# Two score groups ahead of a tile's value chunks, another place for the modulation lines, and another order of VectorE's statistics, in an attention and FP4 feed-forward block

## What is computed

```python
mod = (silu(c) @ wmod).reshape(B, 6, 1, D)
sa, ca, ga, sb, cb, gb = (mod[:, i] for i in range(6))
ga, gb = (gates pushed away from zero, to at least 0.25 in size)
h = layernorm(x) * (1 + ca) + sa
q, k, v = h @ query_proj, h @ key_proj, h @ value_proj
sim = einsum('bnkh,bmhk->bnhm', q, k) / 4
attn = softmax(sim, axis=1)                 # over n, the queries
x = x + ga * (attn @ v) @ output_proj
h = layernorm(x) * (1 + cb) + sb
x = x + gb * ffn(h)                         # silu(gate) * up, FP4-rounded operands
```

## Time and profile before

| | us |
|---|---|
| median of 3 runs | 1777.58 (1774.27 to 1778.04) |
| the profiled execution | 1776.08 |
| its span in the profile | 1774.8 |
| TensorE busy | 1687.0 (95%) |
| VectorE busy | 1663.4 (94%) |
| ScalarE busy | 1368.5 (77%) |
| GpSimd busy | 500.3 (28%) |

### The profile page before, as it was taken

How to read it: one execution, slowest core, us unless ns; L and a number is a source line. 1 busy time by engine, 2 the same in 40 slices (tenths; PEclk the granted TensorE clock), 3 DMA queues, 4 the chain that set the end, 5 groups by cost and what they waited for, 6 DMA issues and landing times.

```text
span 1774.8 us, 38040 instructions
## 1 busy us (share of the span) xinstructions
PE 1687.0 (95%) x15114; PEld 805.4 (45%) x15114; DVE 1663.4 (94%) x2356; ACT 1368.5 (77%) x2552; POOL 500.3 (28%) x983
## 2 busy tenths in 40 slices
PE   7999999999999999999999999999999899999996
PEld 6642223222232223753222223222232488989995
DVE  7889999999999999679999999999999699999995
ACT  5389999999999998559999999999999322232322
POOL 3012212212212222002212212212222455666663
PEclk9999999999999999999999999999999999999998
DMA  6102110111111112411011111111112121222100
GB/s 222 60 2 62 39 45 31 31 34 39 38 43 31 32 31 60 134 43 38 31 33 39 39 44 31 32 34 39 38 43 89 55 71 67 73 72 82 62 13 18
DMA packets 53020, 89.55 MB, mean 50 GB/s; under 512 B 3298, under 2 KB 34922, under 8 KB 52842
## 3 DMA queue, kind: packets, MB, share of 16 engines
q1 hardware_dynamic: 52426, 86.59, 15.1%
q10 hardware_dynamic: 416, 0.53, 0.1%
HBM read 57.74 MB, written 29.37 MB: 49 GB/s over the span
## 4 chain that ended last, share of the span: by engine, by line
PE 51%; ACT 21%; issue 13%; DVE 11%; POOL 2%; SPq 1%; DMA 1%; DVEq 0%; POOLq 0%; ACTq 0%
PE acc L569 25%; ACT e_sb L760 20%; PE slot L540 8%; PE acc L408 7%; PE slot L408 6%; PE acc L589 4%; DVE e_sb L1092 1%; DVE nm L1004 1%; SPq L310 1%; PE slot L630 1%; DVE e_sb L1091 1%; DVE e_sb L1087 1%; DMA mod_rows<-v_sb 1%; DVE ost L1015 1%; DVE st L862 1%
## 5 line engine op out<-in xcount | busy, mean ns | idle before, releaser
L1004 DVE TENSOR_REDUCE nm<-slot 128x1 f32<-128x1024 f32 x1024 | 1181.3, 1214 | 13.1 <-PE slot L540 13.1
L760 ACT ACTIVATE e_sb<-slot,nm 128x1024 f32<-128x1024 f32 x1024 | 1140.2, 1113 | 30.4 <-DVE nm L1004 28.3
L569 PE MATMUL acc<-e_sb,vp 64*64 64x512 f32 x8192 | 1065.1, 593 | 40.2 <-ACT ost L782 38.6
L540 PEld LDWEIGHTS slot<-stq,stk 64*64 64x64 f16 x4096 | 118.4, 103 | 663.0 <-ACT e_sb L760 619.7
L540 PE MATMUL slot<-stq,stk 64*64 64x512 f16 x4096 | 417.7, 392 | 0.0
L569 PEld LDWEIGHTS acc<-e_sb,vp 64*64 64x64 f32 x8192 | 283.2, 133 | 191.4 <-issue 92.4
L1242 POOL TENSOR_TENSOR dlt<-nm 128x4 f32<-128x4 f32 x128 | 25.4, 198 | 712.5 <-DVE nm L1004 712.5
L760 ACT ACTIVATION_READ_ACCUMULATOR e_sb<-slot,nm 128x1 f32 x1024 | 197.3, 193 | 0.0
L1233 POOL TENSOR_TENSOR vp<-v_sb,fac 128x512 f32<-128x512 f32 x128 | 133.4, 1042 | 10.4 <-POOL fac L1223 0.7
L805 ACT COPY e_sb<-slot 128x256 f32<-128x256 f32 x32 | 11.9, 373 | 160.9 <-PE slot L600 160.9
L851 POOL TENSOR_TENSOR hqT_lo<-e_sb,hqT_hi 128x640 fp32r<-128x640 f32 x64 | 115.8, 1829 | 50.3 <-ACT hqT_hi L683 50.3
(11 more groups left out here) (167 smaller groups left out, 1754.9 us busy)
## 6 DMA issues: line engine op xcount, KB each, us to landing
stk<-qk_parts SPq DMA_DIRECT2D x128, 128.0 KB
o_heads<-ost SPq DMA_DIRECT2D x64, 256.0 KB, 3.4
v_sb<-o_heads SPq DMA_DIRECT2D x8, 2048.0 KB, 8.7
v_sb<-in_x SPq DMA_DIRECT2D x16, 512.0 KB, 7.4
qk_parts<-e_sb SPq DMA_DIRECT2D x32, 256.0 KB, 2.3
stq<-qk_parts SPq DMA_DIRECT2D x128, 64.0 KB
out<-e_sb SPq DMA_DIRECT2D x32, 128.0 KB, 1.7
v_sb<-in_wgu SPq DMA_DIRECT2D x1, 1408.0 KB, 14.3
```

Source lines behind the costliest of these rows:

```text
L540: mm = pe.matmul(slot[s][side * VD:(side + 1) * VD, c * 512:(c + 1) * 512], stk[c * 64:c * 64 + 64, h % 2, i * P + side * VD:i * P + (side ...
L569: mm = pe.matmul(acc[half * VD:(half + 1) * VD, c * 512:(c + 1) * 512], vp[rows, g % 3, gi, half, :], e_v[rows, j % ERING, n0:n0 + 512], s ...
L760: act.activation(e_v[:, j % ERING, half * 1024:(half + 1) * 1024], slot[u % 3][:, :], ACT.Exp, bias=nm[:, g % 4, i, half:half + 1], accum_ ...
L1004: dve.tensor_reduce(nm[:, g % 4, i, half:half + 1], slot[u % 3][:, :], AX.X, ALU.max, negate=True).then_inc(maxed.sem)
```

## The change

Four edits. (1) `mrow` moves from 9216 to 12288, the place of value tile 12; `tmp` stays. The wait for the store moves from tile 9 to tile 12 on both engines, and ScalarE's copy of tile 10 waits for the finished lines, since `tmp` lies there. (2) In attention, the two score groups of a tile come ahead of both value chunks on TensorE, and on ScalarE both exponentials come ahead of the copy of chunk 0. VectorE's order there (maximum, maximum, copy) stays. (3) In batch 0's preparation `low_tokens(0, 1)` comes ahead of `stats(0, 3)`, and `normalise(0, 3)` behind the fourth part of group 0. (4) Between the batches VectorE's order is statistics 0 and 1, normalisation 0 and 1, statistics 2, low part 0, statistics 3, normalisation 2 at JT + 2, and low part 1 and normalisation 3 at JT + 6.

```diff
--- before.py
+++ after.py
@@ -171,7 +171,7 @@
         w_xn = ost[:, :, :].rearrange("p a b -> p (a b)")[:, 0:1408]
         w_big = vp[:, :, :, :, :].rearrange("p a b c d -> p (a b c d)")[:, 0:1408]
         wm = region(v_sb, 4480, 2, 1536)
-        mrow = region(v_sb, 9216, 4, D)
+        mrow = region(v_sb, 12288, 4, D)
         tmp = region(v_sb, 10240, 2, D)
         x_v = region(v_sb, 0, NT, D)
         hT_at = [4096, 6144, 12288, 14336]
@@ -659,10 +659,11 @@
                     for half in range(2):
                         if j < JT:
                             scores(b, j, half)
-                        if j < NT - EARLY:
-                            values(b, EARLY + j, half)
                         if j >= LAG:
                             attend(b, 2 * (j - LAG) + half)
+                    if j < NT - EARLY:
+                        for c in range(2):
+                            values(b, EARLY + j, c)
                     if b + 1 < B and j in (JT + 3, JT + 5):
                         turn_tokens(b + 1, (j - JT) // 2 - 1)
             for i in range(TILES + 6):
@@ -712,7 +713,9 @@
                 act.wait_ge(*normalised(b, NG - 1))
             if b == 0 and i == 4:
                 act.wait_ge(*rows_mm.past(1))
-            if b == 0 and i == EARLY:
+            if b == 0 and i == 10:
+                act.wait_ge(*rows_made.past(1))
+            if b == 0 and i == 12:
                 act.wait_ge(*rows_out.past(0))
             act.copy(v_sb[:, i * HV:i * HV + 512], quarter_of(b, "v", 2 * tile)).then_inc(v_act.sem)
 
@@ -782,12 +785,12 @@
                         act.copy(ost[:, h % 2, 512:1024], acc[:, 512:1024]).then_inc(took_high.sem)
                     if j < JT:
                         exponent(b, j, half)
-                    if half == 0 and j < NT - EARLY:
-                        take_values_act(b, EARLY + j)
                     if half == 0 and j % GROUP == 0 and GROUP <= j <= JT:
                         g = j // GROUP - 1
                         act.wait_ge(*diff_cut.past(b * JG + g))
                         act.activation(cor[:, g % 4], dlt[:, g % 4], ACT.Exp).then_inc(cor_made.sem)
+                if j < NT - EARLY:
+                    take_values_act(b, EARLY + j)
                 if j == JT + 2 and b == B - 1:
                     act.wait_ge(*vp_made.past(B * JG - 1))
                     for k in range(2):
@@ -981,8 +984,9 @@
                     part_dve(b, g, r)
                     if b == 0 and g == 0 and r == 1:
                         normalise(0, 2)
+                        low_tokens(0, 1)
                         stats(0, 3)
-                        low_tokens(0, 1)
+                    if b == 0 and g == 0 and r == 3:
                         normalise(0, 3)
                     if b == 0 and g == NG - 1:
                         weight_step(b, step)
@@ -1026,13 +1030,17 @@
                 if j < NT - EARLY:
                     take_values_dve(b, EARLY + j)
                 if j == JT + 2 and b + 1 < B:
-                    for g in range(0, NG, 2):
-                        stats(b + 1, g)
-                        stats(b + 1, g + 1)
-                        normalise(b + 1, g)
-                        normalise(b + 1, g + 1)
-                if j in (JT + 5, JT + 6) and b + 1 < B:
-                    low_tokens(b + 1, j - JT - 5)
+                    stats(b + 1, 0)
+                    stats(b + 1, 1)
+                    normalise(b + 1, 0)
+                    normalise(b + 1, 1)
+                    stats(b + 1, 2)
+                    low_tokens(b + 1, 0)
+                    stats(b + 1, 3)
+                    normalise(b + 1, 2)
+                if j == JT + 6 and b + 1 < B:
+                    low_tokens(b + 1, 1)
+                    normalise(b + 1, 3)
                 if j == JT + 2 and b == B - 1:
                     dve.wait_ge(*wgu_high.past(1))
                     low(dve, wgu_lo[:, 0, :], wguT[:, 0, :], wgu_hi[0][:, :])
```

## The result

The changed kernel takes 1771.75 us (median of 7 runs, 1770.21 to 1774.96) against 1777.58 for the kernel before (7 runs, 1773.79 to 1779.02). The ratio is 0.9973, with an interval of 0.9962 to 0.9985: faster by 4.8 us, between 2.7 and 6.8 (the medians alone differ by 5.8). A second measurement of ten runs on another occasion gave 0.9974 [0.9964, 0.9983]. The forecast was 1770.6, between 1766.5 and 1774.5. Executions that took over 3 ms (two of one variant, one of the kernel before) are left out of the medians and ratios given here.

The account below looks back on a forecast made before the run. No engine owned the last-ending chain; VectorE and ScalarE were nearly always busy in the long stage, which no edit touches. Terms -4.3 - 1.5 - 1.6 + 0.4 = -7.0 us gave 1770.6 against the median, range 1766.5 to 1774.5.

Parts of the forecast that it names:

- The modulation lines: Batch 0's seven tiles: moving the lines from value tile 9 to 12 removes the store wait, -4.3 us (bounds -3.6 and -4.5).
- The place and the cover: Tile 12 becomes first waiter near 93 us, the store lands about 84, leaving cover of some 9 us.
- The first preparation: Batch 0: low part of token group 1 ahead of group 3's statistics starts TensorE earlier, -1.5 us (bounds -0.9 and -1.8).
- The 1.8 us that I drew from that rule: First preparation's gain if GpSimd's root of group 3, by the shared-port rule, takes the short time; 1.0 by the longest row.
- The second preparation: Between the batches: VectorE's new order closes TensorE's whole gap before low part 0, -1.6 us (bounds -1.3 and -1.6).
- The reordered tiles: Seven tiles per batch, scores before both value chunks: +0.2 us a batch, +0.4 in all (bounds -2.8 to +2.8).
- The cycle: Reordered tiles: a turn through TensorE, VectorE and ScalarE's copy takes 7.78 us for two tiles, 3.89 a tile.
- The rival with TensorE as the bound at 3.64 us a tile: Reordered tiles: TensorE sets the pace, 3.64 instead of 3.89 us, giving 3.5 us more, 1767.1; chance 0.08.
- another rhythm: Long stage locks into a slower alternation, 0.02 us more per half tile, costing 20 us, 1791; chance 0.04.
- given back in the weight steps: Preparation gains are lost in VectorE's full queue of weight quantisation, 1773.7; chance 0.07.

## Why the prediction was right

**The modulation lines (-4.3).** The traces give -4.45, and the edit alone 4.1 us by the median. The place and the cover were right: the store is issued at 71.99 in the changed kernel and its landing never shows; ScalarE copies tile 12 at 92.71 (forecast near 93), and with VectorE's orders alone the wait for the store ended at 83.95 (forecast about 84). The size was in part luck. Of the 4.3 us, about 1.5 were the clock's fall behind the wait (31.50 against 29.96 us from the first score to the last copy in the two traces of before), which happened in two of four traces. The bounds of this term, -3.6 to -4.5, missed that: the second trace of before puts the term at 29.96 - 27.17 = 2.8. ScalarE's idle time was no lower bound: it idled 3.43 us there, and 0.6 of that was made up afterwards.

**The first preparation (-1.5).** -1.35 in the first trace. In all seven traces with the new order the first score comes 51.3 us behind the start of the low part of group 1, in the four with the old one 51.5, so both ends do hang together as forecast. That start was 27.06 before. It was 25.91 here and not 25.6, as ScalarE had its input later: TensorE's clock came up later in this trace (last 0.63 us product at 20.69 instead of 20.01). In the second trace of the changed kernel it came up earlier (19.60), and the gain over the first trace of before is 1.80 us:

```profile
25.46 1.23 DVE L854 TENSOR_TENSOR hT_lo<-e_sb,hT_hi 128x1024 fp32r<-128x1024 f32 x1 [0.20 <-ACT hT_hi L695]
...
76.77 0.63 PE L540 MATMUL slot<-stq,stk 64*64 64x512 f16 x8
```

The first score lies at 76.61 to 78.12 us in the seven traces and at 78.43 to 78.98 in the four; the means differ by 1.5. So the new order gains the forecast's size in the mean, and what it gains in one execution goes with the clock at the start. In the first trace the rest of the order came out as written, with VectorE's low part of group 2 at 31.59 (forecast 31.3) and its first weight step at 42.25, 1.33 us earlier. GpSimd's root of group 3 beside the parts took the short time, as the Trainium skill's page "SBUF — State Buffer", section "SBUF: two separate sides", would have it, against 1.91 in the earlier trace rows:

```profile
29.15 1.01 POOL L1190 TENSOR_TENSOR rstd<-ve,mhalf 128x4 f32<-128x4 f32 x1 [5.61 <-DVE ve L870]
```

The 1.8 us that I drew from that rule did not follow in the first trace, because ScalarE had become the last to arrive, at 25.88 us. In the second it arrives last too, but at 25.43, and the gain is there.

**The second preparation (-1.6).** -1.69 in the first trace. TensorE's first query product of batch 1 stands at 707.69, behind attended products that end at 707.76, with no gap.

**The reordered tiles (+0.4).** Up to VectorE's last copy 27.05 and 27.31 us in the first trace, the latter with the lower clock at its start, and 27.03 and 27.02 in the second; 27.17 before. With 0.2 to 0.3 us at each entry of the long stage that is +0.1 a batch at the full clock, +0.2 in all. The cycle was right to 0.01 us, and TensorE's waits in it are where I put them, on ScalarE's v_sb copy. The rival with TensorE as the bound at 3.64 us a tile was wrong for this kernel, and its size was nearly right (3.51) once the copy had moved.

**The other rivals.** The long stage did not take another rhythm: 586.64 to 586.76 us in every trace, whatever came before it. That rival's count was off, which changes little: the stage has 497 maxima, one each 1.18 us, not 505 at 1.15. Nothing was given back in the weight steps.

**The sum.** Up to the feed-forward, where the change ends, the first traces differ by 5.6 us; without the 1.6 us that the clock took at the down weights and in the tiles behind them it is 7.2, against 7.0. But this comparison has the clock's price of 1.5 us in the kernel before. The second traces have no fall in either kernel ahead of the feed-forward and differ by 6.5 (1399.45 and 1392.98), of which 2.2 are the first preparation, with its late clock in the one and its early clock in the other. At the full clock and with the mean of the first preparation the terms are -2.8 - 1.5 - 1.7 + 0.2 = -5.8. The timed runs say 4.8 [2.7, 6.8], which agrees with 5.8 better than with 7.0. So the mechanisms were right and the forecast was too large by the clock's price in the trace that I worked from. What is left, about 1 us, is within the interval. The mean recorded clock of the ten later timed runs is 0.9938 for the changed kernel and 0.9948 for the twenty of before in the same comparison. Whether the changed order loses more to the clock on average, or ten runs are too few, stays open; it was not tested.

## What to carry to other kernels

A change of order on the busiest engine pays only if the hand-overs around it are moved with it: walk one full turn of the loop over all engines, sum the distances from start to start as the trace has them, and compare it with the engine's own work. Here one copy on an engine with time to spare decided between 3.89 and 3.51 us a tile. Where a buffer is borrowed for a store, what counts is when the store lands behind everything queued ahead of it, so borrow a place that is wanted late enough. And a stall's price read from one trace may hold a clock change that the next execution doesn't have; a second trace of the same kernel tells.

## What the hardware showed that I had not expected

Behind one wait of 2.58 us in the same place of the program, TensorE's clock fell in three traces of nine and stayed in the others, and it did the same behind the modulation wait: 0.95 and 1.00 granted in the same stretch of two traces of one kernel. Such falls account for 1.4 to 1.7 us each ahead of the feed-forward, and the feed-forward itself varied between 373.1 and 378.9 us, in mean granted clock between 0.98 and 0.97. The moment at which the clock first comes up varies too: the last product of 0.63 us starts between 19.46 and 22.39 us in the eleven traces. With it the first score varied by 1.5 us under the new order of the first preparation, and by 0.6 under the old. An 8 KB store issued behind sixteen stack loads kept its waiters until 11.8 us after its issue (73.37 to 85.17); I take the transfers ahead of it for the cause, which was not tested. Two score groups in a row take 0.63 us against 0.41 for one, so the second adds 0.22, and a tile of TensorE's own work went from 3.88 to 3.51 us when each kind of product came in one piece.
